# Second attention of a two-layer kernel: the values products in four bursts a step instead of six

## The reference, cut to what matters

```python
def _L1_attn_ref(x, wq, wk, wv, wo):
    B, T, C = x.shape
    q = (x @ wq).reshape(B, T, N_HEADS, HEAD_DIM)
    k = x @ wk
    v = x @ wv
    scores = jnp.einsum('bqhd,bkd->bhqk', q, k) * scale
    scores = jnp.where(causal[None, None], scores, -jnp.inf)
    probs = jax.nn.softmax(scores.astype(jnp.float32), axis=-1).astype(x.dtype)
    out = jnp.einsum('bhqk,bkd->bqhd', probs, v).reshape(B, T, C)
    return out @ wo
```

## Time and profile before

| | us |
|---|---|
| median of 3 runs | 2156.2 |
| lowest and highest | 2155.67, 2158.36 |
| the profiled execution | 2149.3 |
| its span | 2147.5 |
| second attention within it, about | 1495 to 2022 |

### The profile page before, as it was taken

The page is one execution under the profiler, slowest core; times in us unless marked ns, Lnnn a source line. Parts: engine busy times, 40 slices in busy tenths (PEclk is TensorE's granted clock), DMA queues, the critical chain, the costliest instruction groups (busy, mean ns, idle before and its releaser), DMA issues. The chain is left out here.

```text
span 2147.5 us, 34578 instructions
## 1 busy us (share of the span) xinstructions
PE 1968.2 (92%) x12776; PEld 1173.9 (55%) x12776; DVE 1174.7 (55%) x2557; ACT 903.5 (42%) x1909; POOL 524.4 (24%) x408
## 2 busy tenths in 40 slices
PE   5859999999999999999977899997999999999698
PEld 4535666666666666666643454554444444444277
DVE  3546655555555555555402455446676776675078
ACT  3413344444444444444430122221666656666344
POOL 0014235555434443555330000000000000000143
PEclk9869999999999999999998999995999999999599
DMA  9752233222233323322235221144132132220121
GB/s 310 258 155 60 61 80 81 70 58 57 69 81 80 80 71 80 80 67 59 56 107 189 66 67 48 58 113 125 22 53 47 33 53 45 35 38 18 33 87 59
DMA packets 113594, 172.21 MB, mean 80 GB/s; under 512 B 26186, under 2 KB 46826, under 8 KB 113298
## 3 DMA queue, kind: packets, MB, share of 16 engines
q1 hardware_dynamic: 112402, 169.75, 29.9%
q10 hardware_dynamic: 1024, 0.26, 0.1%
HBM read 84.32 MB, written 29.38 MB: 53 GB/s over the span
## 5 line engine op out<-in xcount | busy, mean ns | idle before, releaser
L886 ACT ACTIVATE at_prob<-at_scp 128x512 f32<-128x512 f32 (+1 forms) x608 | 349.7, 576 | 512.2 <-PE at_scp L989 511.0
L1659 ACT ACTIVATE as_prob<-as_scp 128x512 f32<-128x512 f32 (+2 forms) x640 | 309.0, 563 | 200.3 <-PE as_scp L1769 148.9
L921 DVE CUSTOM_DVE_ANT_0 at_junk<-at_mxp,causal 128x128 f32<-128x128 f32 (+3 forms) x512 | 243.4, 488 | 188.6 <-PE at_mxp L1000 183.9
L1709 DVE TENSOR_REDUCE as_mxd<-as_mxp 128x2 f32<-128x256 f32 (+3 forms) x256 | 202.6, 820 | 98.3 <-PE as_mxp L1788 96.1
L916 DVE TENSOR_REDUCE at_mxf<-at_mxp 128x1 f32<-128x512 f32 x256 | 175.9, 687 | 141.3 <-PE at_mxp L1000 137.4
L1694 POOL TENSOR_TENSOR l_att_t<-l_att_t,as_spread 64x1024 f32<-64x1024 f32 x16 | 37.9, 2367 | 863.2 <-DMA as_spread<-l_recips 863.2
L1707 DVE TENSOR_REDUCE as_mxf<-as_mxp 128x2 f32<-128x1024 f32 x128 | 151.0, 1221 | 52.8 <-PE as_mxp L1783 52.6
L816 POOL TENSOR_TENSOR at_pre<-at_prob 128x512 f32<-128x512 f32 x64 | 80.1, 1281 | 407.2 <-ACT at_prob L886 407.2
L816 POOL TENSOR_TENSOR at_pre<-at_pre,at_prob 128x512 f32<-128x512 f32 x128 | 160.3, 1282 | 3.6 <-ACT at_prob L886 1.2
L1807 PE MATMUL as_op<-as_prob,l_vn 128*32 128x512 f32 (+3 forms) x1536 | 160.4, 540 | 0.0
L1022 PE MATMUL at_op<-at_prob,l_cn 128*32 128x512 f32 (+3 forms) x1536 | 143.7, 491 | 4.0 <-ACT at_u_sb L857 4.0
(11 more groups left out here) (248 smaller groups left out, 3480.5 us busy)
## 6 DMA issues: line engine op xcount, KB each, us to landing
hd_late_q<-at_slo SPq DMA_DIRECT2D x96, 128.0 KB, 2.4
at_qhi<-at_shi SPq DMA_DIRECT2D x96, 128.0 KB, 2.4
at_qlo<-at_slo SPq DMA_DIRECT2D x96, 128.0 KB, 2.5
hd_early_q<-at_shi SPq DMA_DIRECT2D x84, 128.0 KB, 2.5
at_spread<-l_recips SPq DMA_DIRECT2D x64, 128.0 KB, 2.7
l_o<-at_u_sb SPq DMA_DIRECT2D x16, 512.0 KB, 3.3
hd_early<-in_wmod SPq DMA_DIRECT2D x7, 1024.0 KB, 7.4
hd_late<-l_o SPq DMA_DIRECT2D x12, 512.0 KB, 4.1
```

The lines of the kernel that those rows point to most:

```text
L886: nc.scalar.activation(prob[:, x % RING0, c0:HALF], scp[x % BANKS0][:, c0:HALF], ACT.Exp).then_inc(s["exp_done"], 1)
L921: nc.vector.tensor_tensor_reduce(out=junk[:, u % 2, 0:w], in0=tile[:, 0:w], in1=k.causal[:, HALF - w:HALF], scale=1.0, scalar=LOWEST, op0= ...
L1659: nc.scalar.activation(prob[:, x % RING1, cols], scp[x % BANKS1][:, cols], ACT.Exp).then_inc(s["exp_done"], 1)
L1709: nc.vector.reduce_max(mxd[:, t % 2, :, i, qt:qt + 1], tile[:, :, 0:(qt % 4 + 1) * P], AX_X).then_inc(s["mx_done"], 1)
```

## The change

Only the place of the values in PE's order is changed. A table says behind which quad of a step a burst stands and which quads it takes, counted from the step's first; -4 to -1 are quads 8 to 11 of the step before. The bursts behind quads 3 and 11 are gone: quads 0 and 1 are taken with 2 and 3 behind quad 5, and quads 8 and 9 with 10 and 11 behind quad 1 of the next step. Behind the loop the last four quads are taken. No product, wait or buffer is added or removed.

```diff
@@ -1088,6 +1088,7 @@
 LEAD = MSTEP + 8
 TURN_AT = 9
 QSETS = QUADS * STEPS1
+BURSTS1 = {1: (-4, -3, -2, -1), 5: (0, 1, 2, 3), 7: (4, 5), 9: (6, 7)}
 MXBANKS, BANKS1, RING1 = 2, 3, 24
 UNITS1_OF = [2 if kt - 4 * qc >= 2 else G for qc, kt in QK]
 FIRST1 = [sum(UNITS1_OF[:n]) for n in range(QUADS)]
@@ -1823,10 +1824,10 @@
                             maximum(u)
                         for j in range(2 * i, min(2 * i + 2, UNITS1_OF[n])):
                             score(t, n, j)
-                    if g % 2 and g >= 3:
-                        values(*divmod(g - 3, QUADS))
-                        values(*divmod(g - 2, QUADS))
-                for g in (QSETS - 2, QSETS - 1):
+                    for i in BURSTS1.get(n, ()):
+                        if QUADS * t + i >= 0:
+                            values(*divmod(QUADS * t + i, QUADS))
+                for g in range(QSETS - 4, QSETS):
                     values(*divmod(g, QUADS))
         clear(nc, s)
```

## The result

| | before | after |
|---|---|---|
| median, us | 2157.0 (4 runs, 2155.67 to 2158.36) | 2230.8 (4 runs, 2221.59 to 2234.72) |
| profiled execution | 2149.3 | 2228.3 |
| span | 2147.5 | 2226.5 |

The ratio is 1.0337, with a 95% interval of 1.0308 to 1.0367. The change makes the kernel 74 us slower, where 35 were forecast and 54 was the end of the range. It is slower, as was forecast, but by twice as much.

A forecast was written before the change was run, and what follows sets the result against it. PE was taken to be held to DVE's pace between bursts. Waits of 12.4 and 9.1 us, 1 where maxima are absent and 13.1 for the clock made 35.6 on 2156.2, so 2191 us, range 2169 to 2211.

The forecast's parts named there:

- What bounds the kernel: Second attention: between bursts PE goes at DVE's pace through two maxima banks; a burst of 1.64 us hides DVE's work.
- Place B: Quads 10, 11, 0 and 1: PE waits for reductions, 0.88 us lost behind each of 14 steps, 12.4 us.
- Place A: Quads 2 to 5: 1.07 us lost in 8 steps with DVE's weight split, 0.08 in 7 others, 9.1 us.
- The places taken as nothing: Bursts behind quads 7 and 9, the ring of 24 buffers, copies out of `as_op`, the very end: no cost.
- The clock: Place A, steps 2 to 9: one more drop to 1.2 GHz in each, 8 x 1.64 = 13.1 us.
- third rival: Clock gets much worse, staying down through quads 4 and 5 and the burst, other steps too: 60 us, 2216; chance 0.10.
- In the other steps I leave the number as it is.: Outside steps 2 to 9: number of clock drops unchanged, since the thin stretch of quads 6 and 7 stays.
- the 0.34 us from a maximum to the next scores or mask: Behind a burst, against a steady 0.23: part of 0.31 us a burst in the faster rival, 9.6 us less, chance 0.07.

The follow-up runs named there:

- e8: The kernel before, with DVE's reductions of the maxima over half their columns and exponentials scaled, as a measure only: 2123.2 us, ratio 0.9843.
- e9: The changed kernel, with DVE's reductions of the maxima over half their columns and exponentials scaled, as a measure only: 2148.2 us, ratio 0.9962 to the kernel before.
- e1: The changed kernel, but quads 0 and 1 keep their burst behind quad 3; only that of quads 8 and 9 is moved: 2187.2 us, ratio 1.0154.
- e7: The changed kernel, with the first matmul of 17 of a step's 24 maxima done twice, in every stretch without values: 2188.5 us, ratio 1.0153.
- e4: The kernel with twelve bursts a step, the values of one quad (n-2) behind every quad n: 2271.5 us, ratio 1.0556 to the kernel before.
- e2: The changed kernel, but quads 8 and 9 keep their burst behind quad 11; only that of quads 0 and 1 is moved: 2187.7 us, ratio 1.0160.
- e3: The changed kernel, with DVE's weight split in steps 2 to 9 behind quad 5's maxima instead of quad 2's: 2197.2 us, ratio 1.0205.
- e5: The kernel before, with the first matmul of three of the four maxima of quads 6 and 7 done twice: 2155.1 us, ratio 0.9991.
- e6: The kernel before, with the first matmul of the maxima but the first done twice in quads 4 and 5 and in 6 and 7: 2147.4 us, ratio 0.9955.

## Why the prediction was wrong

**What bounds the kernel**: right. PE is held by DVE between bursts, and the burst is where DVE catches up; e8 and e9 turn the sign of the change at the full clock by halving DVE's reductions.

**Place B**: the mechanism and the times were right to 0.12 us; the price is 0.76 instead of 0.88, and 0.75 by the steps of e1 without a drop. 14 x 0.76 = 10.6 us for 12.4 (14 x 0.88 is 12.3).

**Place A**: right. 9.70 against 9.77 without the split; with it a wait of 1.14 us, worth 1.07 a step by the forecast and 1.06 by the steps of e7 at the full clock, with the split and without. The two terms together are some 19 us for the 21.5 forecast, and PE's waits for DVE rose by 19.9.

**The places taken as nothing** (quads 6 to 9, the ring, the copies) cost no waits in the changed kernel: its list has none for the copies, and that for the exponentials fell from 10.8 to 6.9 us. The warning that the copies keep their places was the right thing to look at, since they are what broke e4.

**The clock is the step that failed.** The forecast was 13.1 us, one more drop of 1.64 us in each of the eight steps with the split, and as an upper bound two in those eight and one in seven others, 37 us. Measured, it is 74 - 19 = 55 us. A drop of 1.64 us is 3.4 us at 1.2 GHz, so the forecast stood for 27 us more at the low level; measured are 153 more. Three things were mis-sized.

- How long a drop is. The 1.64 us were read from drops of 3.4 us that hit a burst of 1.86. In the changed kernel the drops at place A last 6.8 or 10.2 us, through quads 4 and 5 and the merged burst, which goes from 2.29 us to 4.4. The third rival said this; it was given 0.10 and, at 60 us for all, priced too low. By the microsecond the low level costs no more than before: 41.0 - 33.46 = 7.5 for 20.5 us in steps 5 to 9, against 1.64 for 3.4.
- Where there are any. A drop was added at quads 2 to 5 of eight steps only. In the trace place A has one in eleven of steps 1 to 14, 96 us at 1.2 GHz in all. Place B, which the forecast gave none, has one in eleven steps too, 55 us in all. In e2 and e3 place A has a drop in every one of these steps.
- "In the other steps I leave the number as it is." At quad 7 this came out: seven drops before and seven after. But the number is no property of the stretch alone, so that was luck: in e1, with quads 6 and 7 in the same order, there are ten. Nothing shown of the trace of before gives the new number, and the range should have been widened for that.

Two readings of the prediction need a word. Of the four maxima in the stretch ahead of a drop only the last two waited for their bank, by 0.16 and 0.32 us at their weight loads, and not every one. And the 0.34 us from a maximum to the next scores or mask, in which it saw the price of a burst's layout, stand also behind a maximum that had waited, with no burst before it (1578.98 to 1579.32); so the 0.11 us of it are not shown to be the burst's.

The Trainium skill says that the clock is set by how busy TensorE has been ("TensorE: Matmul & The Clock Gate", "What's actually happening"). The runs agree in direction: e7 gives PE more to do in the same stretches, and the time at 1.2 GHz falls from 254 to 94 us. They don't show which measure of busy counts. PE's busy time was 2.96 of 3.30 us ahead of a drop of before, which speaks for the work in the array, but e7 also takes away half of PE's waits for DVE.

What stays open: how the number of drops follows from the order and from the step's length. e1 came out at 23 us of clock for a merge with waits of 0.76 us, and no run here separates its new phase from its longer stretch.

## What to carry to other kernels

Where two engines with shallow buffers sit behind a third, work of the third that needs neither of them is cover. Lumping it saved at most 0.39 us a burst here (e9 against e8), and lost more than that. Cutting it into twelve pieces lost too, through the one bank `as_op` (e4), so a new place for such work has to be checked against every buffer that it shares. If the granted clock of a stretch is under 1.00, look for the thinnest stretch between the dense pieces before moving anything, since here five steps that waits alone made 5.8% longer (33.46 for 31.63 us) came out 30% longer (40.98). Work done twice where the engine waits anyway can be a gain: it was 0.4% here, once quads 4 to 7 had it, nothing when only quads 6 and 7 had, and less again when quad 3 had it too.

## What the hardware showed that was not expected

- The clock's drops can keep step with the loop. In the kernel before they came every second step at the same burst, seven times, 64.8 us apart; in the changed one steps 5 to 9 have their three drops at the same places, and each takes 41.0 us. The length of such a step is not its own work alone.
- Filling one thin stretch took the drops behind it away and brought others elsewhere (e5), 20.5 us at 1.2 GHz in steps 1 to 13 for 23.9. The gain came only when quads 4 and 5 were filled too (e6), and then no drop was left there.
- A wait of 1.1 us a step, 9 us in all, carried 20 to 25 us of clock with it (e3 against the changed kernel). Where e7's clock was kept up, the same wait was worth its 1.06 us a step and no more.
